# Every second load of a weight tile is issued by ScalarE instead of SyncE

## The reference, cut to what matters

```
def ffn(x, weight):                                  # used before and after attn
    alpha = max(mean(abs(weight)), 1e-8)
    w_q   = clip(round(weight / alpha), -1, 1)       # ternary weights
    beta  = max(max(abs(x), axis=-1) / 127, 1e-8)
    x_q   = clip(round(x / beta), -127, 127)
    return einsum('bsi,oi->bso', x_q, w_q) * alpha * beta

def attn(x):                                         # gated linear recurrence
    left  = gelu(x @ Wl + bl)
    u     = causal_conv4(x @ Wr + br)
    r, i  = sigmoid(u @ Wa + ba), sigmoid(u @ Wi + bi)
    a     = exp(-8 * softplus(-lam) * r)
    h_t   = a_t * h_(t-1) + sqrt(1 - a_t**2) * i_t * u_t
    return (left * h) @ Wo + bo

x = x + 0.5 * ffn(layernorm(x), W)
x = x + attn(layernorm(x))
x = x + 0.5 * ffn(layernorm(x), W)
```

## Time and profile before

| | us |
|---|---|
| median of 3 runs | 3457.51 (3456.04 to 3467.17) |
| the profiled execution | 3453.65 |
| its span on the slowest core, core 6 | 3452.1 |
| spans of the other seven cores | 3434.2 to 3449.2 |

### The profile page before, as it was taken

How to read it: one execution, slowest core, us unless ns; L and a number is a source line. 1 busy time by engine, 2 the same in 40 slices (tenths; PEclk the granted TensorE clock), 3 DMA queues, 4 the chain that set the end, 5 groups by cost and what they waited for, 6 DMA issues and landing times.

```text
span 3452.1 us, 28677 instructions; the slowest of 8 cores (3434.2 to 3452.1 us)
## 1 busy us (share of the span) xinstructions
PE 2214.8 (64%) x9734; PEld 963.3 (28%) x9734; DVE 1202.8 (35%) x1601; ACT 747.8 (22%) x817; POOL 118.6 (3%) x145
## 2 busy tenths in 40 slices
PE   0004444444259979992999999991887774454445
PEld 0001222222024434441444444440332221222112
DVE  3665444444000005552335353531110025434443
ACT  0122222223111213331334343430000011111110
POOL 0000000000000000000000000000100000000000
PEclk9997777777679989996999999995998887777778
DMA  5531111121734232317345454526334351111111
GB/s 145 197 134 61 61 61 61 61 81 66 140 72 84 66 70 63 74 49 176 47 68 70 68 70 68 69 50 174 100 97 99 98 171 48 49 74 72 50 49 49
DMA packets 252878, 290.33 MB, mean 84 GB/s; under 512 B 168257, under 2 KB 209217, under 8 KB 240449
## 3 DMA queue, kind: packets, MB, share of 16 engines
q0 software_dynamic: 144816, 111.16, 17.7%
q1 hardware_dynamic: 81762, 135.40, 12.1%
q10 hardware_dynamic: 26160, 41.95, 3.7%
HBM read 239.19 MB, written 98.57 MB: 98 GB/s over the span
## 4 chain that ended last, share of the span: by engine, by line
PE 56%; DMA 13%; DVE 13%; issue 8%; ACT 7%; another core or an unknown queue 2%; DVEq 1%; ACTq 0%; SPq 0%; POOLq 0%; POOL 0%
PE pmm L859 10%; PE pmm L868 10%; PE pmm L574 8%; PE pmm L937 8%; PE pmm L745 8%; PE pmm L797 8%; DMA bigA<-s_zn 2%; DMA s_zn<-stg 2%; PE ptrb L549 2%; PE pmm L943 2%; ACT stg L449 2%; DVE stt L445 2%; DVE stt L442 2%; DMA wg<-Wo 2%
## 5 line engine op out<-in xcount | busy, mean ns | idle before, releaser
L574 PE MATMUL pmm<-bigA,wg 128*128 128x512 bf16 x2048 | 513.1, 413 | 499.1 <-DVE bigB L592 244.5
L574 PEld LDWEIGHTS pmm<-bigA,wg 128*128 128x128 bf16 x2048 | 210.6, 105 | 777.8 <-issue 587.0
L859 PE MATMUL pmm<-bigA,wg 128*128 128x512 bf16 x1600 | 360.5, 381 | 62.3 <-DMA bigA<-s_u 61.5
L937 PE MATMUL pmm<-wg,bigA 128*128 128x512 bf16 x1280 | 296.2, 388 | 141.6 <-DMA wg<-Wo 141.6
L868 PE MATMUL pmm<-bigA,wg 128*128 128x512 bf16 x1600 | 358.4, 379 | 0.0
L745 PE MATMUL pmm<-bigA,wg 128*128 128x512 bf16 x1280 | 278.4, 381 | 109.7 <-DMA bigA<-s_zn 109.7
L817 DVE SCALAR_TENSOR_TENSOR sc<-sc,vecs 128x2048 f32<-128x2048 f32 x60 | 141.1, 2351 | 527.4 <-ACT sc L811 523.3
L797 PE MATMUL pmm<-bigA,wg 128*128 128x512 bf16 x1280 | 280.3, 380 | 21.1 <-DMA wg<-Wr 19.2
L549 PE MATMUL ptrb<-identb,wg 128*128 128x128 bf16 x512 | 105.4, 225 | 286.8 <-DVE wg L533 151.6
L449 ACT ACTIVATE stg<-bigB 128x2048 bf16<-128x2048 f32 x32 | 61.1, 1909 | 1038.6 <-DVE stt L445 965.2
L859 PEld LDWEIGHTS pmm<-bigA,wg 128*128 128x128 bf16 x1600 | 157.0, 98 | 253.1 <-issue 66.0
(11 more groups left out here) (120 smaller groups left out, 1652.0 us busy)
## 6 DMA issues: line engine op xcount, KB each, us to landing
bigB<-WfT SPq DMA_DIRECT2D x32, 1024.0 KB, 6.0
bigB<-xN SPq DMA_DIRECT2D x16, 1024.0 KB, 9.8
bigB<-s_x SPq DMA_DIRECT2D x16, 1024.0 KB, 6.9
s_x<-bigB POOLq DMA_DIRECT2D x7, 2048.0 KB, 7.5
out<-bigB POOLq DMA_DIRECT2D x7, 2048.0 KB, 6.9
wg<-Wa POOLq DMA_DIRECT2D x20, 640.0 KB, 7.3
wg<-Wi POOLq DMA_DIRECT2D x20, 640.0 KB, 7.3
wg<-Wl POOLq DMA_DIRECT2D x5, 2048.0 KB, 17.3
```

The source lines that it names most:

```text
L574: e.matmul(p.t[:], wg[:, xof + i * TB + tb * 128: xof + i * TB + tb * 128 + 128], bigA[:, i * D + os * 512: i * D + (os + 1) * 512], start ...
L859: E.pe(lambda e, off=off, c=c, pr=pr, k=k: e.matmul(pr.t[:], wg[:, off:off + 128], bigA[:, c * T + k * TT: c * T + (k + 1) * TT], start=(c ...
L937: E.pe(lambda e, c=c, tb=tb, p=p: e.matmul(p.t[:], bigA[:, c * T + tb * 128: c * T + tb * 128 + 128], wg[:, c * 512:(c + 1) * 512], start= ...
```

## The change

In both loops the load of an odd tile is issued by ACT, that of an even tile still by SP. Buffers, sizes, the place of the load in the code and all compute instructions stay.

```
@@ alpha loop
-            E.dma("sp", lambda e, c=c, hsl=hsl: e.dma_start(
-                out=bigB[:, hsl], in_=WfT[c * 128:(c + 1) * 128, :]), writes=[b])
+            E.dma("sp" if c % 2 == 0 else "act",
+                  lambda e, c=c, hsl=hsl: e.dma_start(
+                      out=bigB[:, hsl], in_=WfT[c * 128:(c + 1) * 128, :]),
+                  writes=[b])
@@ emit_quant(c)
-            E.dma("sp", lambda e, c=c, hof=hof: e.dma_start(
-                out=bigB[:, hof:hof + D], in_=WfT[c * 128:(c + 1) * 128, :]),
-                writes=[bq])
+            E.dma("sp" if c % 2 == 0 else "act",
+                  lambda e, c=c, hof=hof: e.dma_start(
+                      out=bigB[:, hof:hof + D],
+                      in_=WfT[c * 128:(c + 1) * 128, :]),
+                  writes=[bq])
```

## The result

| | before | changed |
|---|---|---|
| median of 8 runs, us | 3460.6 | 3516.9 (3506.8 to 3527.1) |
| ratio (95% interval) | 1 | 1.0158 (1.0139 to 1.0177) |
| measured once more, beside other kernels | 1 | 1.0145 (1.0125 to 1.0165) |
| profiled execution, us | 3453.65 | 3507.51 |
| alpha loop, first to last reduction, us | 59.9 | 59.5 |

The stage lengths are means over the 8 cores of one profile each, read from the timelines; the alpha loop's is from the start of its first reduction to the start of its last. In some executions the cores of one die have a lower granted clock and the time is several per cent longer (one of the eight of before, 3687 us; the mean of the other seven is 3460.7), so the ratios rest on the other executions, 2 to 10 of each changed kernel. The forecast was slower, 3495 us, range 3482 to 3511. The direction and the place are right; the time lies above the range.

The account below looks back on a forecast made before the run. Waits, not a full engine, set the alpha loop's pace, and the quantisation's end is on the path. 0 - 0.5 + 33.4 + 8.7 = 41.6 us on 3453.65 gave 3495 us, range 3482 to 3511.

Parts of the forecast that it names:

- The alpha loop costs nothing: Alpha loop: a second issuing queue adds no engine, so the seven steps of the chain change by 0.
- queues sharing evenly, +8: Alpha loop: two queues share evenly, each first load lands some 1.2 us later, +8 us, 3504; part of rivals given 0.22.
- the loads slipping out of step, -9: Alpha loop: odd loads slip out of step and land nearer 4.8 than 6.1 us, up to -9; chance 0.12.
- The 0.5 us less at the join: After the alpha loop: tile 1's load is not yet in flight, so the first scaling starts 0.5 us sooner.
- A load behind the store waits in full, at six tiles and tile 7, not at 13: Quantisation: ACT-issued odd loads become waits at tiles 1, 3, 5, 7, 9, 11, 15; tile 13 has 5.9 us to spare.
- Six tiles at 5.6 us, 33.4 us: Quantisation, tiles 1, 3, 5, 9, 11, 15: each pays 5.6 us (4.9 to 7.0), together 33.4 (29 to 42).
- The share of the store in the load's landing, 0.7: Quantisation, odd tiles: the store issued just before delays the load's landing by 0.7 us, bounds 0 and 2.15.
- Tile 7 at 8.7 us: Quantisation: xN's loads go out earlier and share the engines with tile 7's store and load; 8.7 us, bounds 5.6 and 9.9.
- The 0.6 us to land: Quantisation, tile 7: 0.6 us to land added to 7.7 us of data from about 7.6, giving 15.9.
- The dearer rival: Alpha loop queues share evenly, or quantisation loads start only behind the landed store: +8 each, 3504, both 3512; chance 0.22.
- 2.15: Quantisation, odd tiles: upper bound in us of the store's cost to a load that starts only when the store has landed.
- No gain to be had from a second issuer: Alpha loop: issuing costs SP 0.33 us beside a period of 8.75, so a second issuer has nothing to save.

Follow-up runs that it names:

- the parity turned: Changed kernel with the quantisation's even loads issued by ACT and its odd ones by SP; ratio to before 1.0135 (1.0107 to 1.0162).
- the kernel without even stores: Changed kernel without the stores of even tiles, ACT waiting for DVE's last instruction of the tile instead; ratio to before 1.0128 (1.0104 to 1.0152).
- that kernel: Changed kernel with the quantisation's odd load on ACT emitted ahead of the store of the tile before; ratio to before 1.0006 (0.9996 to 1.0017).

## Why the prediction missed its range

*The alpha loop costs nothing.* Right: 59.9 to 59.5 us, and 0.9999 for that half alone. Neither of the rivals placed there (queues sharing evenly, +8, or the loads slipping out of step, -9) shows. The 0.5 us less at the join were a matter of core 6; on the mean of the cores it is 0.1.

*A load behind the store waits in full, at six tiles and tile 7, not at 13.* Right, tile by tile; shown by the waits, by the parity turned, by all loads on ACT, and from the other side by the load put ahead of the store, which takes the whole loss away.

*Six tiles at 5.6 us, 33.4 us.* This term of the sum failed, by 4.6 us. Over the cores the six cost (store-to-scaling less 0.5, mean of 8 cores) 6.2, 7.2, 6.9, 6.25, 5.8 and 5.7 us, together 38.0. Two things were mis-sized. The share of the store in the load's landing, 0.7, is 1.0: I had put half of the store's 1.3 us of data ahead of the load's, and all of it is ahead. With the shorter gap between the issues (0.37) a plain tile comes to 5.8, some 1 us over six tiles. And I took the median landing of the earlier trace rows as the price of each, though a wait on a load pays the mean, with its late ones, and loads that were hidden before could be late without a trace of it. Tiles 11 and 15 are near the 5.6; tiles 3 and 5 hold most of the excess.

*Tile 7 at 8.7 us.* Its mechanism is right (xN 9 us earlier; with xN held back the excess goes), its size is 9.95 on the mean of the cores and 11.4 on core 5, against the bound of 9.9 that I gave it. The 0.6 us to land in that term were read from no row; the loads of the changed kernel landed 0.3 us after the end of their last packet (5.65 and 5.99, medians).

*The sum against the time.* The other step that failed is the base. The forecast was built on the profiled execution, 3453.65, and I called the median of the three runs shown, 3457.51, near enough; over 8 runs it is 3460.6. So of the 21.6 us between 3495.3 and 3516.9, 7.0 are the base (3.9 of them in sight at the time), 5.5 the quantisation and 0.4 the join. The last 8.7 stand in no stage that can be told from scatter: 3460.6 + 47.6 = 3508 would have lain in the range, and the interval of the ratio is 48 to 61 us over before, so its lower end is the quantisation's 47.6 almost alone (the median of the repeat is 3513.8).

*The dearer rival* named a time nearer to it (3504 to 3512), and half of it holds in kind: the load does stand in line behind the store's data on ACT's queue. But it pays 1.0 us for that and not 2.15, and the queues in the alpha loop cost nothing. The range's upper end came from this rival and held nothing for the base or for the spread of a landing time. By its own tile bounds (42 for the six, 9.9 for tile 7) the forecast's range ended at 3505 and not at 3502.

*No gain to be had from a second issuer.* The Trainium skill says (DMA: Bandwidth & Descriptors, section Issuing engines are not separate DMA queues) that DMAs of different engines run on the same 16 DMA engines and that a second issuer saves only the time of issuing. The runs agree: 0.9999 in the alpha loop, and a landing of 4.7 us on either queue.

**Open.** Why some loads behind a store land after 7 to 8 us. The DMA view of core 5, tile 3, from issue to landing (the rows: rate in 40 slices, queues with packets, MB, share):

```profile
GB/s 0 0 145 436 311 415 415 436 249 207 436 270 83 124 207 539 249 373 415 166 498 539 166 498 415 83 42 41 41 0 41 41 0 41 0 41 41 0 0 0
...
q10 hardware_dynamic: 288, 1.57, 58.0%
q14 instruction: 1, 0.01, 0.3%
```

The bulk is there after some 5 us, and the last 2.5 us carry a thin, even trickle.

```profile
147.50:148.50 1.00, 0.00 (x0) 0.00 (x0) 0.00 (x0) 0.00 (x0) 0.00 (x0) 1.00 0.81 344
148.50:151.00 2.50, 0.00 (x0) 0.00 (x0) 0.00 (x0) 0.00 (x0) 0.00 (x0) 1.00 0.07 26
```

A share of 0.07 is about one of 16 engines, and 26 GB/s over 2.5 us are 65 KB, a sixteenth of the load: it looks as if one engine began its part late, and the load is as late as that engine. Other loads are late in another way. This is the middle of tile 5's load on core 2, which took 8.0 us.

```profile
168.30:172.30 4.00, 0.00 (x0) 0.00 (x0) 0.00 (x0) 0.00 (x0) 0.00 (x0) 1.00 0.88 240
```

All engines are at work there, and the rate is 240 GB/s where one load had 406: each packet took longer (506 ns, against 374 in the median load).

A packet of instructions (q14) is in the window of the first and not of the second. Of the 55 odd loads with nothing of SP's queue in their window, over the 8 cores, 16 had such a packet, with a median landing of 7.0 us (5.9 to 8.1), and 39 had none, with 5.8 (5.4 to 8.0). That does not carry far. In the second profile of the same kernel both medians are 6.1 us (15 loads with a packet, 41 without). In the kernel without even stores the eight loads with a packet landed after 4.7 to 5.5 us. In the kernel with the quantisation's half alone no packet is in the window of tile 3, where all 8 cores had one, and its loads landed after 5.8 us on the mean instead of 7.2; but tile 5's fell as well, from 6.9 to 5.8, with no packet in either kernel. What makes a load late stays open.

## What to carry to other kernels

Before a DMA is handed to another engine, write down what stands ahead of it in that engine's stream and when that is released. The price is the landing time less the lead that the new place leaves, and here one place further up was worth all of it. What was issued just before on the same queue moves its data first, and a landing time read alone does not hold that. A transfer that becomes a wait is to be priced with the mean and the late ones of its landing times beside its new neighbours, not with the median that it had while hidden. And the sum is to be put on the median of the runs, not on the one profiled execution.

## What the runs showed of the hardware

- A load of 1 MB landed after a median of 4.7 us on SP's queue and on ACT's, when nothing else was in flight (core 2 of the kernel without even stores). With a store of 0.5 MB issued 0.4 us ahead on the same queue it took 5.9 on that core.
- On ACT's queue the data of a load came behind those of the store issued 0.4 us ahead: first packet 1.95 us after the issue instead of 0.97, at least 94% of the store's packets started by then (55 loads).
- ACT issued a DMA that stood behind an activation as that activation started (145.34 and 145.35), not when it ended; so in all 64 loads of that kernel's 8 cores, 0.01 to 0.07 us after the start.
- A load can be 2 to 3 us late with one sixteenth of its data still to come (26 GB/s for the last 2.5 us), or with all engines at work on slower packets (506 ns instead of 374).
